# A graph network kernel: source table in four chunks instead of five, and layer 0 selecting ten columns of a block instead of eleven

## The chip, the cores and the metric

The kernel runs on one core of a Trainium2 chip. The metric is the device time of one execution in microseconds. Three runs of the kernel before gave 5798.82, 5797.19 and 5807.0 us, a median of 5798.82 us.

## The reference, cut to what matters

12,500 nodes carry 16 features each; 400,000 edges, sorted by destination, each name a source and a destination node. Two layers run one after the other, and both have the same skeleton: fetch the source row of every edge, turn it into a message, sum the messages by destination.

```
x  = layernorm(x + L0(x));  x = layernorm(x + L1(x))
L0: ew  = (edge_attr @ W_e + b_e).reshape(E, 16, 16)
    msg = einsum('ei,eio->eo', x[src], ew)
    out = segment_sum(msg, dst) / max(count, 1) + bias
L1: msg = einsum('emh,eh->em', edge_emb[edge_type], x[src])
    m   = segment_sum(msg, dst);  out = GRU(m, x)
```

## The kernel before, in words

The edges are worked in 125 blocks of 3200. A block is 25 columns of 128 edges, one edge to a partition. Each layer goes through all 125 blocks, and each block needs `x[src]` for its 25 columns. There are two ways of getting a column, and the kernel uses both at once.

A **gathered** column is one indirect DMA issued by GpSimd (POOL, line 500), 128 rows of 16 numbers straight into the tile `z`. In the kernel before 14 of the 25 columns are gathered.

A **selected** (or picked) column is computed. The node table lies in SBUF as a high and a low part (`table_hi`, `table_lo`), partition p holding the 98 nodes 98p to 98p+97, its groups. For each edge ScalarE (ACT) makes a one-hot column that says which partition holds the source: `dist` (line 570) is the absolute distance between the wanted partition number and the partition, `pick` (line 578) is relu(1 - dist). The 98 groups are cut into chunks of `NG` groups, and the one-hot is made once for every chunk, so that an edge outside a chunk contributes zero. TensorE (PE) multiplies the one-hots with the chunks (line 752), for each chunk once with the high and once with the low part, all accumulated in one PSUM bank: NG groups times 16 features. VectorE (DVE) multiplies that bank with a one-hot over the group inside the chunk (`select`, line 953, two columns at a time, output `cand`) and adds up along the groups (line 959), into `z`. `group_hot` (line 943) makes the group one-hot. Eleven columns of a block are selected, in the order of `PICKED`; ACT works them in two halves (`HCUT`), of 5 and 6 columns.

With the 25 source columns in `z`, DVE forms the outer products of the edges in three parts (`outer`, line 991, after columns 8, 15 and 25), PE sums them by destination in 50 matmul records (`sum_block`, line 789), ACT copies the sums (line 590), PE transposes them (lines 760 to 764), ACT copies again (lines 555, 557), PE multiplies by the weights (lines 770 to 773), and DVE adds the result to the node table by four small additions at addresses it loads into registers (`rows_of_windows`: load at 997, additions at 935).

The work of neighbouring blocks is woven by hand. While block b is summed, PE selects the columns of block b+1: in layer 0 it does columns 0 to 4, then `sum_block(b)`, column 5, the transposes, column 6, the result, and the rest; in layer 1 columns 0 to 2, `sum_block(b)`, 3, 4, the transposes, 5, 6, the result, and the rest (`S_AT`, `T_AT`, `R_AT`). The products go through a ring of six PSUM banks, so column t waits until DVE has taken the column six before it; columns 0 and 1 of the next block wait for the pair (6, 8) of this one. DVE in layer 0 runs, in this order: third outer product of b, pair (0,2) of b+1, the block's destination one-hot (`match_block`), pair (2,4) and its sum, first outer product of b+1, pair (4,6) and its sum, second outer product of b+1, register loads and additions for b, pair (6,8), pair (8,10) and their sum, the single column 10 and its sum, `group_hot`. Layer 1 is the same, with the second outer product after the additions.

The gathers are spread by hand too: `AFTER_OWN`, `AFTER_LAST` and `AFTER_SUMS` name the gathers of a block that wait until PE has finished a given column or `sum_block`.

Of the kernel before, what the change touches and what calls it, by code (L numbers as in the profile page):

```python
# [18 lines left out]
LN_AT = (0, 12, 34, 56, 78, 98)  # L19
N_LN = len(LN_AT) - 1  # L20
PICKED = [4, 5, 6, 7, 13, 14, 21, 22, 23, 24, 20]
H = ((11, 11), (11, 11))
HM = max(max(h) for h in H)
SCUT = [[[sum(p < START[j] for p in PICKED[:h]) for j in range(NS + 1)] for h in hs] for hs in H]
HCUT = [[(0, 5, h) for h in hs] for hs in H]
NH = 2
# [6 lines left out]
S_AT, T_AT, R_AT = (4, 2), (5, 4), (6, 6)  # L33
GATHERED = [[[[g for g in range(START[j], START[j + 1]) if g not in PICKED[:h]] for j in range(NS)] for h in hs] for hs in H]
assert all(2 * n % RING == 0 and n >= max(hs) for n, hs in zip(TURN, H))
HALF_1 = 5
MADE_0 = (H[0][0], HALF_1)
FIRST_GATHERED = [[[g for g in range(START[j], START[j + 1]) if g not in PICKED[m:h[0]]] for j in range(NS)] for m, h in zip(MADE_0, H)]
# [2 lines left out]
SUMMED = [(0, 4), (4, 6), (6, 10), (10, 11)]  # L41
assert all(PICKED[t] == PICKED[a] + t - a for a, b in SUMMED for t in range(a, b))
PAIRS = [[[(t, min(t + 2, h)) for t in range(0, h, 2)] for h in hs] for hs in H]
AFTER_OWN = ([{5: 0, 6: 1, 7: 2, 8: 3, 12: 5, 13: 6}] * 2, [{6: 0, 7: 1, 10: 3, 11: 4, 13: 5}] * 2)
AFTER_SUMS = (9, 8)
AFTER_LAST = ([{0: 7, 1: 8, 2: 9, 4: 10}] * 2, [{0: 7, 1: 8, 2: 9, 4: 10}] * 2)
SUB = 4
GPAD = -(-G // SUB) * SUB
WN = 32
TC, NG = 5, 20  # L50
CHUNKS = (0, 1, 4, 2, 3)
PER_ROW = 98
ROW_MUL, ROW_SHIFT = 2675, 17
NG_MUL, NG_SHIFT = 205, 12
NG_LAST = PER_ROW - (TC - 1) * NG
assert 0 < NG_LAST <= NG and NG_LAST % 2 == 0 and CHUNKS[0] != TC - 1 != CHUNKS[-1] and all(n * NG_MUL >> NG_SHIFT == n // NG for n in range(PER_ROW))
BLK = P * G
# [10 lines left out]
def build(nc, x, src, src_pick, dst, dst_rows_in, ea, etype, W_e, b_e, bias, A_t, w_ihT, w_hhT, b_ih, b_hh, out):  # L68
# [42 lines left out]
    with ExitStack() as ctx:  # L111
# [198 lines left out]
        def picked_of(k, buf, r, n):  # L310
            return ahead(k, buf, r) + H[k][1] + n

        def cand_of(k, buf, r, n):
            return ahead(k, buf, r) + RING + n
# [12 lines left out]
        def windows_of(eng, b):  # L327

            _, (n_win,) = nc.values_load_multi_w_load_instructions(
                span_row[0:1, bass.ds(b, 1), N_WIN:N_WIN + 1].rearrange("p a b -> p (a b)"), [eng.engine], min_val=0,  # L330
                max_val=N_MAX, skip_runtime_bounds_check_because="a count, worked out from the destinations")
            return n_win
# [149 lines left out]
        def _(pool):  # L482
            def gathers(k, table):
                l = L[k]

                def body(b, buf, r, columns):
# [3 lines left out]
                    for j in range(NS):  # L490
                        for g in columns[j]:
                            if b > 0:
                                if n in AFTER_OWN[k][buf]:
                                    pool.wait_ge(l["picked"], picked_of(k, buf, r, AFTER_OWN[k][buf][n] + 1))
                                if n in AFTER_LAST[k][buf]:
                                    pool.wait_ge(l["picked"], picked_of(k, 1 - buf, r - 1 + buf, AFTER_LAST[k][buf][n] + 1))
                                if n == AFTER_SUMS[k]:
                                    pool.wait_ge(l["mm"], b)
# [47 lines left out]
        def _(act):  # L546
            def evacuate(k):
# [11 lines left out]
                def pick_half(b, buf, r, j):  # L559

                    n, lo, hi = TC * (NH * b + j), HCUT[k][buf][j] * P, HCUT[k][buf][j + 1] * P

                    def distances():
                        if isinstance(b, int) and b == 0:
                            act.wait_ge(s_first, 32)
                        else:
                            act.wait_ge(l["src"][buf][j], 16 * (r + buf))
                        for i, c in enumerate(CHUNKS):
                            act.wait_ge(l["pick_act"], n + i + 2 - TC)
                            act.activation(dist[i][:, 0:hi - lo], src_mod[buf][:, lo:hi],  # L570
                                           ACT.Abs, bias=neg_node[:, c:c + 1]).then_inc(l["dist"], 1)

                    def picks(*turns):
                        for i in turns:
                            if i == 0:
                                act.wait_ge(l["picked"], picked_of(k, 1 - buf, r - 1 + buf, HCUT[k][1 - buf][j + 1]))
                            act.wait_ge(l["dist"], n + i + 1)
                            act.activation(pick[j][:, CHUNKS[i], 0:hi - lo], dist[i][:, 0:hi - lo], ACT.Relu,  # L578
                                           bias=1.0, scale=-1.0).then_inc(l["pick_act"], 1)

                    return distances, picks
# [10 lines left out]
                def first_sums(b):  # L592
                    act.wait_ge(l["mm"], b + 1)
                    sums_to_sbuf(l["mS"])

                def first_rows(b):
                    sums_to_rows(l["tp"], l["tS"], b)

                def sums_of_windows(n_win):
                    def window(x, q):  # L600
                        act.wait_ge(l["mm_x"], x + 2)
                        sums_to_sbuf(l["mS_x"])
                        sums_to_rows(l["tp_x"], l["tS_x"], x)

                    with act.If(n_win > 1):
                        for_each_window(act, n_win, extra, window)
# [21 lines left out]
                def body(b, buf, r):  # L628
                    more1 = not (isinstance(b, int) and b + 1 >= NB)
                    more2 = not (isinstance(b, int) and b + 2 >= NB)  # L630
                    n_win = windows_of(act, b)
                    if more1:
                        _, second = pick_half(b + 1, 1 - buf, r + buf, 1)
                    if more2:
                        distances, picks = pick_half(b + 2, buf, r + 1, 0)
                    if more1:
                        second(*range(TC))
                    if more2:
                        distances()
                        if k == 0:  # L640
                            picks(0, 1)
                    first_sums(b)
                    if more2:
                        picks(*((2,) if k == 0 else (0, 1)))
                    first_rows(b)
                    if more2:
                        picks(*((3, 4) if k == 0 else (2, 3, 4)))
                    if more2:
                        distances, _ = pick_half(b + 2, buf, r + 1, 1)
                        distances()  # L650
                    sums_of_windows(n_win)

                return begin, lambda: for_each_block(act, first_body, body)

            def h_to_rows():
# [72 lines left out]
        def _(pe):  # L728
            def sums(k):
# [7 lines left out]
                def pick_rows(b, buf, r, t):  # L737
# [5 lines left out]
                    else:  # L743
                        last = max(u for u in range(H[k][1 - buf]) if (u - t - TURN[k]) % RING == 0)
                        pe.wait_ge(l["cand"], cand_of(k, 1 - buf, r - 1 + buf, last + 1))
                    for i, c in enumerate(CHUNKS):
                        if at == 0:
# [587 lines left out]
```

## Time and profile before

| | us |
|---|---|
| median of three runs | 5798.82 |
| profiled execution, own time | 5833.2 |
| profiled execution, span | 5831.4 |
| PE busy | 5227.1 (90%) |
| PEld busy | 4693.1 (80%) |
| DVE busy | 4199.3 (72%) |
| ACT busy | 3891.8 (67%) |
| POOL busy | 3412.9 (59%) |

The profile is of one execution. PE is TensorE's matmuls and PEld its weight loads, which overlap the matmuls. "q" behind an engine's name is its sequencer. Layer 0 fills the span to about 2890 us, layer 1 runs from about 2970 us. "remote" in a wait, and "another core or an unknown queue" in the chain, is a release for which the profile found no finished instruction just before it.

### The profile page before, as it was taken

The page shows a single profiled execution, that of the slowest core. Times are in us where ns is not written, and L with a number is a line of the kernel's source. Part 1 is how long each engine was busy: PE and PEld are TensorE (multiplying, and loading weights), DVE is VectorE, ACT ScalarE, POOL GpSimd, SP SyncE. Part 2 cuts the span into 40 slices and gives each one's busy share as a digit, 9 for nine tenths or more (in the row PEclk, how much of TensorE's full clock was granted, in tenths as well). Part 3 has the DMA queues.
Part 4 walks back from the last instruction along what each step waited for, and adds up shares of the span by engine and source line. Part 5 has one row for each costly group of instructions (what it writes and reads, how often), then busy time and mean ns, then how long its engine had stood idle before and what let it go on. Part 6 is the DMA issues. An engine that isn't in the chain of part 4 may idle for free.

```text
span 5831.4 us, 131035 instructions
## 1 busy us (share of the span) xinstructions
PE 5227.1 (90%) x41758; PEld 4693.1 (80%) x41759; DVE 4199.3 (72%) x5387; ACT 3891.8 (67%) x5533; POOL 3412.9 (59%) x3559
## 2 busy tenths in 40 slices
PE   6999999999999999999978888888888888888887
PEld 5888888888888888888767878788877788788887
DVE  7878787778777788777856666666666666666666
ACT  6666676676666666666566666666666666666664
POOL 6555565555555555555555656655655655655554
PEclk9999999999999999999989999999999999998998
DMA  3111111111111111111111111111111111111110
GB/s 66 33 30 31 33 31 31 31 31 33 30 31 33 30 31 33 31 32 31 25 23 23 23 24 23 23 23 22 23 23 23 23 23 22 24 22 23 23 23 14
DMA packets 330970, 161.25 MB, mean 28 GB/s; under 512 B 193244, under 2 KB 330011, under 8 KB 330771
## 3 DMA queue, kind: packets, MB, share of 16 engines
q1 hardware_dynamic: 218224, 130.59, 9.3%
q0 software_dynamic: 112512, 29.03, 6.3%
q10 hardware_dynamic: 160, 0.80, 0.1%
q8 instruction: 27, 0.44, 0.0%
q14 instruction: 47, 0.39, 0.0%
HBM read 157.44 MB, written 2.66 MB: 27 GB/s over the span
## 4 chain that ended last, share of the span: by engine, by line
PE 63%; issue 15%; DVE 12%; another core or an unknown queue 6%; DVEq 4%; ACT 0%; DMA 0%; POOL 0%; SPq 0%; ACTq 0%
PE psN L752 46%; PE psM L789 15%; DVE cand L953 6%; DVEq L997 2%; DVE nodeT L935 2%; DVE z L991 2%; DVE z L959 1%; DVEq L934 1%; DVEq L952 0%; PE psN L893 0%; PE psM L764 0%; DVEq L958 0%; PE psM L773 0%; DVE grp_hot L943 0%
## 5 line engine op out<-in xcount | busy, mean ns | idle before, releaser
L752 PE MATMUL psN<-table_hi,pick 128*128 128x320 f32 (+1 forms) x13670 | 4080.1, 316 | 167.8 <-DVE cand L953 85.3
L752 PE MATMUL psN<-table_lo,pick 128*128 128x320 f32 (+1 forms) x13670 | 3987.4, 308 | 13.7 <-issue 13.7
L752 PEld LDWEIGHTS psN<-table_hi,pick 128*128 128x128 f32 x13670 | 2598.8, 190 | 306.4 <-issue 226.1
L578 ACT ACTIVATE pick<-dist 128x640 fp32r<-128x640 bf16 (+1 forms) x2485 | 1790.5, 784 | 1336.8 <-PE psN L752 852.8
L752 PEld LDWEIGHTS psN<-table_lo,pick 128*128 128x128 f32 x13670 | 2599.6, 190 | 21.6 <-issue 21.5
L500 POOL DMA_INDIRECT z<-in_x,idx x1761 | 1704.4, 968 | 1176.9 <-issue 417.4
L500 POOL DMA_INDIRECT z<-h_rows,idx x1755 | 1682.2, 959 | 1168.3 <-issue 403.7
L570 ACT ACTIVATE dist<-src_mod,neg_node 128x640 bf16<-128x640 uint16 (+1 forms) x2485 | 1972.6, 874 | 3.3 <-DMA src_mod<-src_mod_rows 3.3
L953 DVE TENSOR_TENSOR cand<-psN,grp_hot 128x640 f32<-128x640 f32 (+1 forms) x1492 | 1122.1, 765 | 1061.3 <-PE psN L752 482.7
L991 DVE TENSOR_TENSOR z<-psD,z 128x2048 f32<-128x2048 f32 (+1 forms) x750 | 1367.8, 1824 | 55.6 <-issue 31.5
L789 PE MATMUL psM<-z,onehot 128*32 128x273 f32 (+1 forms) x12500 | 904.4, 345 | 371.4 <-issue 327.0
L959 DVE TENSOR_REDUCE z<-cand 128x64 f32<-128x1280 f32 (+2 forms) x995 | 1064.5, 1070 | 85.6 <-DVE cand L953 0.5
L789 PEld LDWEIGHTS psM<-z,onehot 128*32 128x32 f32 x12500 | 484.4, 111 | 746.7 <-issue 643.3
L935 DVE TENSOR_TENSOR nodeT<-nodeT,psM 17x32 f32 (+1 forms) x1000 | 178.6, 179 | 383.7 <-remote 220.2
L590 ACT COPY sumS<-psM 128x273 f32<-128x273 f32 (+1 forms) x250 | 82.0, 328 | 407.9 <-PE psM L789 407.4
L968 DVE TENSOR_TENSOR onehot<-col_f,psD 128x800 f32<-128x800 f32 x250 | 244.7, 979 | 0.0
L555 ACT COPY sumT<-psM 128x384 f32<-128x384 f32 x125 | 60.2, 482 | 123.0 <-PE psM L761 121.2
L943 DVE TENSOR_TENSOR grp_hot<-col_f,grp 128x220 f32<-128x220 f32 x249 | 94.5, 379 | 0.2
L770 PE MATMUL psM<-sumT,W 128*128 128x128 f32 x500 | 76.0, 274 | 2.3 <-issue 1.7
L770 PEld LDWEIGHTS psM<-sumT,W 128*128 128x128 f32 x500 | 69.9, 190 | 2.7 <-issue 1.9
L973 DVE COPY psD<-eab 128x400 f32<-128x400 f32 x125 | 71.3, 570 | 0.0
L773 PE MATMUL psM<-sumT,A 128*128 128x128 f32 x250 | 48.1, 274 | 0.7 <-issue 0.4
(108 smaller groups left out, 734.3 us busy)
## 6 DMA issues: line engine op xcount, KB each, us to landing
src_mod<-src_mod_rows SPq DMA_DIRECT2D x249, 192.0 KB
src_mod<-src_mod_rows SPq DMA_DIRECT2D x248, 160.0 KB
z<-in_x,idx POOLq DMA_INDIRECT x1761
z<-h_rows,idx POOLq DMA_INDIRECT x1755
eab<-in_edge_attr SPq DMA_DIRECT2D x125, 200.0 KB
idx<-in_src SPq DMA_DIRECT2D x250, 12.5 KB
dstb<-in_dst SPq DMA_DIRECT2D x250, 14.0 KB
grp<-src_grp SPq DMA_DIRECT2D x249, 5.5 KB
```

The costliest lines, as they stand in the source:

```text
L500: pool.indirect_dma_start(xs[k][buf][:, g, :], None, table, bass.IndirectOffsetOnAxis(ap=idx[buf][:, g:g + 1], axis=0),).then_inc(l["got"] ...
L570: act.activation(dist[i][:, 0:hi - lo], src_mod[buf][:, lo:hi], ACT.Abs, bias=neg_node[:, c:c + 1]).then_inc(l["dist"], 1)
L578: act.activation(pick[j][:, CHUNKS[i], 0:hi - lo], dist[i][:, 0:hi - lo], ACT.Relu, bias=1.0, scale=-1.0).then_inc(l["pick_act"], 1)
L752: mm = pe.matmul(rows[:, :, 0:cells.shape[2]], pick[j][:, c, at:at + P], cells, start=(i == 0 and part == 0), stop=(i == TC - 1 and part = ...
L770: pe.matmul(psR[:, 0:P], W0[:, c, :], sumT[:, c, :], start=(c == 0), stop=False)
L789: mm = pe.matmul(psM[s * WN:(s + 1) * WN, 0:W], onehot[buf][:, g, :], z[k][buf][:, g, 0:W], start=(g == FIRST_POS[s]), stop=(g == LAST_POS ...
L935: return dve.tensor_tensor(v, v, psR[p0:p1, s * WN:(s + 1) * WN], ALU.add).then_inc(acc, 1)
L953: dve.tensor_tensor(cand[:, t0 - g0:t1 - g0], psN[:, a:a + m, 0:NG * F].rearrange("p m (f g) -> p m f g", g=NG), grp_hot[:, t0:t1, :].unsq ...
L959: dve.tensor_reduce(xs[k][buf][:, PICKED[t0]:PICKED[t1 - 1] + 1, :], cand[:, t0 - g0:t1 - g0], AX.X, ALU.add).then_inc(l["sel"], t1 - t0)
L968: return dve.tensor_tensor(onehot[buf][:], col_f[:, 0:WN].unsqueeze(1).to_broadcast([P, G, WN]), bc(rel[buf][:, 0:G], WN), ALU.is_equal)
L991: dve.tensor_tensor(z[k][buf][:, cs, 0:n * F].rearrange("p g (k i) -> p g k i", i=F), coef[k][buf][:, cs, :].unsqueeze(3).to_broadcast([P, ...
L997: _, vals = nc.values_load_multi_w_load_instructions(span_row[0:1, bass.ds(b, 1), 0:N_WIN + 1].rearrange("p a b -> p (a b)"), [dve.engine] ...
```

## The change

The 98 groups are cut into four chunks of 26, 26, 26 and 20 groups (before: four of 20 and one of 18), in the order 0, 3, 1, 2. Layer 0 selects the first ten columns of `PICKED` and gathers fifteen; layer 1 keeps eleven and fourteen. The points at which gathers wait follow the new counts. ACT's split of the chunks in layer 0 (before: two, one, two) becomes two, one, one.

```diff
-H = ((11, 11), (11, 11))
+H = ((10, 10), (11, 11))
-AFTER_OWN = ([{5: 0, 6: 1, 7: 2, 8: 3, 12: 5, 13: 6}] * 2, [{6: 0, 7: 1, 10: 3, 11: 4, 13: 5}] * 2)
-AFTER_SUMS = (9, 8)
-AFTER_LAST = ([{0: 7, 1: 8, 2: 9, 4: 10}] * 2, [{0: 7, 1: 8, 2: 9, 4: 10}] * 2)
+AFTER_OWN = ([{4: 0, 5: 1, 6: 2, 7: 3, 9: 4, 12: 5, 13: 6}] * 2, [{6: 0, 7: 1, 10: 3, 11: 4, 13: 5, 14: 6}] * 2)
+AFTER_SUMS = (10, 8)
+AFTER_LAST = ([{0: 7, 1: 8, 2: 9}] * 2, [{0: 7, 1: 8, 2: 9, 4: 10}] * 2)
-TC, NG = 5, 20
-CHUNKS = (0, 1, 4, 2, 3)
+TC, NG = 4, 26
+CHUNKS = (0, 3, 1, 2)
-NG_MUL, NG_SHIFT = 205, 12
+NG_MUL, NG_SHIFT = 158, 12
-                        picks(*((3, 4) if k == 0 else (2, 3, 4)))
+                        picks(*range(3 if k == 0 else 2, TC))
```

## Rows read from the trace of the kernel before

**Rows 1.** The page's chain that ended last, shares of the span.

```profile
PE 63%; issue 15%; DVE 12%; another core or an unknown queue 6%; DVEq 4%; ACT 0%; DMA 0%; POOL 0%; SPq 0%; ACTq 0%
```

**Rows 2.** Busy time in two stretches, layer 0 and layer 1.

```profile
100.00:2870.00 2770.00, 2613.36 (x20461) 2299.29 (x20460) 2205.44 (x2543) 1895.38 (x2662) 1634.79 (x1696) 1.00 0.17 31
3000.00:5780.00 2780.00, 2438.62 (x20010) 2243.68 (x20014) 1809.24 (x2579) 1850.55 (x2681) 1643.20 (x1715) 0.97 0.14 23
```

**Rows 3.** Waits, 200 to 2800 us: total us, times, longest.

```profile
POOL z L500 <- issue: 375.3, 1162, 2.7
...
DVE nodeT L935 <- remote: 191.8, 112, 2.5
DVE cand L953 <- remote: 135.5, 85, 2.6
```

**Rows 4.** Waits, 3100 to 5700 us.

```profile
DVE cand L953 <- remote: 189.6, 88, 2.8
...
PEld psM L789 <- DVE z L991: 35.9, 46, 0.9
...
PE psN L752 <- ACT pick L578: 24.3, 25, 1.1
```

**Rows 5.** Groups of instructions with shapes apart: busy us, mean ns.

```profile
L953 DVE TENSOR_TENSOR cand<-psN,grp_hot 128x640 f32<-128x640 f32 x1242 | 999.0, 820 | 1010.0 <-PE psN L752 458.0 <-remote 355.9 <-issue 195.3
...
L959 DVE TENSOR_REDUCE z<-cand 128x64 f32<-128x1280 f32 x497 | 739.0, 1487 | 51.1
...
L959 DVE TENSOR_REDUCE z<-cand 128x32 f32<-128x640 f32 x248 | 203.6, 821 | 25.9 <-DVE cand L953 0.5
...
L953 DVE TENSOR_TENSOR cand<-psN,grp_hot 128x320 f32<-128x320 f32 x250 | 123.0, 492 | 51.3 <-PE psN L752 24.7
```

**Rows 6.** The page's costliest groups: ACT's two steps and the gathers.

```profile
L578 ACT ACTIVATE pick<-dist 128x640 fp32r<-128x640 bf16 (+1 forms) x2485 | 1790.5, 784 | 1336.8 <-PE psN L752 852.8
L500 POOL DMA_INDIRECT z<-in_x,idx x1761 | 1704.4, 968 | 1176.9 <-issue 417.4
...
L570 ACT ACTIVATE dist<-src_mod,neg_node 128x640 bf16<-128x640 uint16 (+1 forms) x2485 | 1972.6, 874 | 3.3 <-DMA src_mod<-src_mod_rows 3.3
```

**Rows 7.** Timeline of layer 0, PE: start, duration; first matmuls of two neighbouring columns.

```profile
1506.30 0.31 PE L752 MATMUL psN<-table_hi,pick 128*128 128x320 f32 x1
...
1507.74 0.31 PE L752 MATMUL psN<-table_hi,pick 128*128 128x320 f32 x1
```

**Rows 8.** Timeline of layer 0, from column 5 to the next block's column 0.

```profile
1502.70 0.82 DVE L953 TENSOR_TENSOR cand<-psN,grp_hot 128x640 f32<-128x640 f32 x1 [0.91 <-PE psN L752]
...
1504.49 2.02 DVE L991 TENSOR_TENSOR z<-psD,z 128x1792 f32<-128x1792 f32 x1
...
1504.64 0.39 PE L771 MATMUL psM<-sumT,W 128*128 128x128 f32 x2
...
1508.65 1.13 DVE L935 TENSOR_TENSOR nodeT<-nodeT,psM 17x32 f32 x4 [2.14 <-remote]
...
1510.07 1.56 DVE L953 TENSOR_TENSOR cand<-psN,grp_hot 128x640 f32<-128x640 f32 x2 [0.29 <-issue]
...
1511.05 0.41 PE L752 MATMUL psN<-table_hi,pick 128*128 128x320 f32 x1 [0.26 <-DVE cand L953]
```

**Rows 9.** The block before: DVE's sequencer past its wait for the result (line 933).

```profile
L933 DVEq FUSED_REGOPS  x1: 46/46/46, 1485.2 to 1485.2; - x1
```

**Rows 10.** The same block: PE's sequencer at the next body's first register load.

```profile
L329 PEldq TENSOR_LOAD <-dst_mem x1: 305/305/305, 1485.3 to 1485.3; - x1
```

**Rows 11.** Timeline of a block in layer 1.

```profile
4479.77 0.41 PE L752 MATMUL psN<-table_hi,pick 128*128 128x320 f32 x1 [0.60 <-issue]
...
4484.82 0.42 PE L789 MATMUL psM<-z,onehot 128*32 128x128 f32 x8 [0.47 <-issue]
...
4489.34 0.41 PE L752 MATMUL psN<-table_hi,pick 128*128 128x320 f32 x1
...
4491.15 0.82 DVE L953 TENSOR_TENSOR cand<-psN,grp_hot 128x640 f32<-128x640 f32 x1 [3.19 <-PE psN L752]
...
4497.07 0.82 DVE L953 TENSOR_TENSOR cand<-psN,grp_hot 128x640 f32<-128x640 f32 x1 [2.25 <-remote]
```

## The prediction

> **What bounds the kernel now.** I read the chain that ended last first, then the busy times by layer, then the waits, then one block of each layer in order of time. In the chain PE has 63%, but DVE has 12% and 6% go to releases that the profile cannot name [rows 1]: a PE that was simply the limit would not need these. The busy times say which layer is which. A block of layer 0 has 169 matmul records (110 for the table, 50 sums, 9 behind them), so its stretch of 2770 us holds 20461/169 = 121.1 blocks of 22.88 us, with PE busy 21.6 and DVE 18.2 us of each; layer 1 has 163, hence 122.8 blocks of 22.64 us, with PE 19.9 and DVE 14.7 [rows 2]. PE is nearly full in layer 0, less so in layer 1.
>
> One block of layer 0 shows a loop. PE finishes column 5, DVE takes pair (4,6) at 1502.70, starts the second outer product at 1504.49, the additions at 1508.65, pair (6,8) at 1510.07, and only then, at 1511.05, may PE start column 0 of the next block [rows 8]. So the block is set by DVE's path behind column 5, not by PE's columns, which stop for 0.26 us there. Inside that path DVE stands idle 2.14 us before the additions although PE ended the result at 1504.64 + 0.39 = 1505.03 [rows 8]. This wait comes in nearly every block: 191.8 us over 112 times, and a second one ahead of a pair costs 135.5 us in 85 times [rows 3]. It looks as if the release of PE's semaphore came late. What it coincides with: in the block before, DVE got past the wait at 1485.2, and at 1485.3 PE's sequencer had run to the first register load of the next body [rows 9, 10]. I read this as: while PE's sequencer is pushing columns it lets no release out, and it lets them out when it has pushed the last one.
>
> The Trainium skill ("PSUM — Partial Sum Buffer", Engine vs sequencer instructions) says that an update attached to a matmul fires when that matmul completes. The rows disagree by 3.4 us in the place just shown. By that rule the additions would be held by something else, and fewer columns behind the result would not bring them forward.
>
> **The change part by part.**
>
> *PE, fixed cost of a matmul.* A column is ten matmuls and takes 1.44 us [rows 7]. It streams 98 groups x 16 x 2 = 3136 columns either way, 1307 ns at the granted clock of 1.00 (2.4 GHz) [rows 2]; the other 133 ns are 13 ns a matmul. Eight matmuls instead of ten save 0.027 us: 10 x 0.027 = 0.27 us a block in layer 0, 0.30 in layer 1. Bounds: nothing, if the 13 ns grow with width, and twice that.
>
> The Trainium skill ("TensorE: Matmul & The Clock Gate", Back-to-back issue gap) gives a fixed 2.5 ns for a warm matmul. By it the saving would be 0.05 us a block, some 13 us over both layers in place of 71; the row, 13 ns, is what I use.
>
> *PE, the eleventh column of layer 0* goes: 1.41 us more. Together 1.7 us a block, 212 us over 125 blocks, if PE were the only limit.
>
> *DVE, wider pairs.* A pair grows from 640 to 832 elements. From 492 ns at 320 and 820 at 640 the slope is 1.03 ns an element, so +0.20 us a pair; the sum of four columns goes from 1280 to 1664 elements at (1487 - 821)/640 = 1.04 ns, +0.40 us, that of two +0.20 [rows 5]. Layer 0: five pairs 0.99, sums 1.00, less the single column and its sum (0.49 + about 0.49): net +1.0 us a block. Layer 1: 1.09 + 1.10 = +2.2 us a block. `group_hot` adds under 0.1 us to either. DVE is then busy 19.2 of about 22 us, and 16.9.
>
> *ACT* makes two one-hots fewer a block, each 0.87 + 0.78 us: 3.3 us less of about 15 [rows 2, 6]. It pays where PE waits for ACT: 24.3 us in layer 1 [rows 4]. Elsewhere ACT waits for PE, and it is worth nothing.
>
> *POOL* issues one gather more in layer 0. A gather is 0.97 us and about 0.32 us to the next [rows 3, 6], so fifteen take 19.4 us of a block of about 22. The new waits tie it to PE columns, and the one on `sum_block` moves to the eleventh gather. With 2.6 us of slack I cost it at nothing; without that cover it would cost up to 1.3 us a block, 160 us. SP's loads are unchanged in number.
>
> **Sum for layer 0.** The path from column 5 to the next column 0 is 8.35 us (1502.70 to 1511.05), of which 2.14 is the late release. Three steps on it grow by 0.20: 8.95 us if the release stays where it is, 6.8 if it no longer counts. With the eleventh column gone PE's sequencer reaches the end of the body 1.4 us and more earlier, and DVE arrives 0.4 later, so I expect most of the 2.14 to vanish. PE itself needs for column 6, result and three columns 8.2 - 1.5 = 6.7 us, which meets the path at about the same point. That is worth 8.35 - 6.8 = 1.5 us. Against it stands the second late release, inside `sum_block`, 135.5 us in all [rows 3]: nothing in the change moves it, and behind it DVE has one pair and one four-column sum more to carry (+0.6). Between no gain (both releases stay) and 1.7 us (PE alone decides) I take 1.0 us: -125 us.
>
> **Sum for layer 1.** Here the sums wait for the third outer product: column 0 starts at 4479.77, the sums at 4484.82, though three columns need 4.3 us; the sums end at 4489.34, pair (2,4) follows at 4491.15, pair (4,6) at 4497.07 after a late release of 2.25 [rows 11]. So the loop is outer product, sums, column 3, DVE's whole remaining list, outer product. The 2.2 us of wider DVE work lie on it almost entirely. What can absorb them is the late release, 189.6 us in about 117 blocks, 1.6 us a block [rows 4], if it comes earlier or DVE simply arrives later. That leaves 2.2 - 1.6 = 0.6, less 0.2 for the waits for ACT [rows 4]: +0.4 us a block, +50 us. Bounds: -0.3 (PE's own saving, all else absorbed), -38 us, and +2.2, +275 us.
>
> Together 5833.2 - 125 + 50 = 5758 us for the profiled execution, which is 34.4 us above the median of the runs; **5724 us** as a median.
>
> **The rivals.**
>
> *A. PE's saving comes through whole.* Both late releases move with the shorter pushing of PE's sequencer, since every column has four instructions fewer in twenty. For it: PE is busy 94% in layer 0 [rows 2]. Against: DVE's path. Layer 0 -1.6 us a block, layer 1 none: -200 us, 5599.
>
> *B. Slower: DVE's list in layer 1 is the bound.* Mechanism: the loop through the third outer product and `sum_block`. For it: the sums already wait for DVE, 35.9 us in 46 times and the 0.47 us in [rows 4, 11]; all the 2.2 us are on the loop. It decides if the release ahead of pair (4,6) stays late relative to column 3, so that only the work in front of it hides: then +1.4 us a block, +175 us, while layer 0 keeps only 0.6 us, -75 us. Total +100: 5899. A lower clock adds to it: in layer 1, with PE busy 88%, the granted clock averages 0.97 against 1.00 in layer 0 at 94% [rows 2], and an emptier PE could be given that in layer 0 too.
>
> *C. The two layers cancel.* Layer 0 gains 0.6, layer 1 loses 0.6 us: 5799.
>
> **How the numbers follow.** Forecast 0.38, A 0.22, B 0.32, C 0.08. The predicted time is the forecast's, with a range of its own of 5670 to 5780. For 8 in 10 the range goes from just above the middle of A to the middle of B: 5595 to 5895. A measurement tells 0.2%, about 12 us, from no change. Faster: the forecast, A: 0.60. Same: 0.07. Slower: 0.33, B and the wrong side of C.
>
> **What would show it.** Pairs at about 1.02 us and four-column sums at 1.89 us confirm the DVE terms; a column at 1.41 us the PE term. In layer 0 the "remote" wait ahead of the additions should fall from 1.7 us a block to under 0.5, and the block to about 21.9 us. In layer 1 the wait of the sums for the outer product should grow and the block be about 23.0 us. The forecast is wrong if the remote waits of layer 0 stay, if POOL's gathers hold an outer product, or if the granted clock in layer 0 drops below 0.97.

## The result, and the profile after

The changed kernel takes 5827.73 us (median of 17 runs, 5820.51 to 5837.6) and the kernel before 5807.0 us beside it (median of 17, 5795.6 to 5823.21). The ratio is 1.0031, with a 95% interval of 1.0021 to 1.0041: slower by 0.3%, little but clear of the noise. Forecast were 5724 us and a chance of 0.33 for slower; the time lies inside the range for 8 in 10 (5595 to 5895) and outside the forecast's own (5670 to 5780). The profiled execution took 5832.04 us (span 5830.2), the one before 5833.2, so the two profiles show how time moved between the layers, and not the 0.3%.

| | before | after |
|---|---|---|
| median | 5807.0 | 5827.73 |
| PE busy | 5227.1 | 5078.8 |
| DVE busy | 4199.3 | 4598.4 |
| ACT busy | 3891.8 | 3059.0 |
| POOL busy | 3412.9 | 3503.1 |
| layer 0, us a block | 22.88 | 23.41 |
| layer 1, us a block | 22.64 | 22.10 |

The chain that ended last, answering to [rows 1]: less of it is without a name, more is PE.

```profile
PE 69%; DVE 14%; issue 13%; DVEq 2%; another core or an unknown queue 1%; ACT 1%; POOL 0%; DMA 0%; ACTq 0%; SPq 0%
```

The busy times by layer, answering to [rows 2]. The first row is layer 0, the second layer 1; the columns are the stretch, its length, then PE, PEld, DVE, ACT and POOL busy with their counts, the granted clock, the DMA share and GB/s.

```profile
100.00:2800.00 2700.00, 2436.09 (x16031) 1984.56 (x16029) 2214.05 (x2191) 1367.39 (x2072) 1642.59 (x1728) 0.99 0.16 30
...
3050.00:5700.00 2650.00, 2291.54 (x16910) 2088.43 (x16910) 2031.54 (x2522) 1472.90 (x2162) 1609.56 (x1684) 0.99 0.14 24
```

A block of layer 0 now has 80 + 50 + 9 = 139 matmul records, so the stretch of 2700 us holds 16031/139 = 115.3 blocks of 23.41 us; one of layer 1 has 88 + 53 = 141, hence 119.9 of 22.10 us. Layer 0 lost 0.53 us a block and layer 1, which was to lose, won 0.54. All block times below come from such a row in the same way (169 and 163 records with five chunks).

The groups with shapes apart, answering to [rows 5], and PE's columns, answering to [rows 7] (total and mean ns stand behind the bar).

```profile
L752 PE MATMUL psN<-table_hi,pick 128*128 128x416 f32 x7830 | 2862.0, 366 | 248.1 <-DVE cand L953 139.0 <-DVEq L920 37.3 <-ACT pick L578 37.1
...
L953 DVE TENSOR_TENSOR cand<-psN,grp_hot 128x832 f32<-128x832 f32 x1242 | 1247.5, 1020 | 869.0 <-PE psN L752 605.2 <-remote 151.9 <-issue 100.8
...
L959 DVE TENSOR_REDUCE z<-cand 128x64 f32<-128x1664 f32 x497 | 937.8, 1887 | 51.2
```

```profile
1500.68 0.31 PE L752 MATMUL psN<-table_hi,pick 128*128 128x320 f32 x1
...
1502.14 0.31 PE L752 MATMUL psN<-table_hi,pick 128*128 128x320 f32 x1
```

DVE's pairs are 1.02 us and its four-column sums 1.89, as the prediction had them. A column takes 1502.14 - 1500.68 = 1.46 us, where the prediction had 1.41 and the kernel before 1.44.

The waits from 200 to 2750 us, answering to [rows 3], which go to 2800 us; the sums' wait of the kernel before, over the same 2550 us, stands in the second fence.

```profile
ACT sumS L590 <- PE psM L789: 502.9, 103, 6.5
...
PEld psM L789 <- issue: 377.6, 640, 1.3
...
DVE cand L953 <- PE psN L752: 334.1, 215, 4.2
...
PE psM L789 <- issue: 142.6, 261, 1.0
...
PE psN L752 <- issue: 29.7, 60, 1.1
...
DVE nodeT L935 <- remote: 8.0, 26, 1.0
DVE cand L953 <- remote: 3.9, 4, 1.5
```

```profile
PEld psM L789 <- issue: 256.3, 475, 1.3
```

The two late releases of layer 0 did go: 191.8 + 135.5 us before, 11.9 after. But the block did not get shorter. The time stands inside `sum_block` (line 789), where PE now stops between matmuls for "issue", with nothing before it that the profile names as a cause. One block of layer 0 in order of time, answering to [rows 8]:

```profile
1488.42 4.54 PE L789 MATMUL psM<-z,onehot 128*32 128x273 f32 x47
...
1489.40 0.95 POOL L500 DMA_INDIRECT z<-in_x,idx  x1 [1.71 <-PE psN L752]
...
1490.66 0.95 POOL L500 DMA_INDIRECT z<-in_x,idx  x1 [0.30 <-issue]
1490.81 0.11 PEld L789 LDWEIGHTS psM<-z,onehot 128*32 128x32 f32 x1 [0.41 <-issue]
1491.54 0.16 PEld L789 LDWEIGHTS psM<-z,onehot 128*32 128x32 f32 x5 [0.62 <-issue]
1491.92 0.95 POOL L500 DMA_INDIRECT z<-in_x,idx  x1 [0.30 <-issue]
1492.29 0.15 PEld L789 LDWEIGHTS psM<-z,onehot 128*32 128x32 f32 x4 [0.60 <-issue]
...
1493.04 0.11 PEld L789 LDWEIGHTS psM<-z,onehot 128*32 128x32 f32 x1 [0.59 <-issue]
1493.18 0.95 POOL L500 DMA_INDIRECT z<-in_x,idx  x1 [0.30 <-issue]
1493.75 0.65 PE L789 MATMUL psM<-z,onehot 128*32 128x273 f32 x3 [0.79 <-issue]
```

The reader is to see four gathers issued while PE sums, and PE's weight loads that come in small groups with about 0.6 us of nothing between them. The 50 records fill 1488.42 to 1494.40. From here on "sums" is the time from the first matmul of line 789 to the first matmul behind `sum_block`, a mean over the blocks of a layer that I worked out from PE's records; so is the number of gathers issued from 1 us before them to 1 us before their end, called the gathers beside the sums. In layer 0 the sums went from 5.19 to 6.62 us (mostly three gathers before, mostly four after); in layer 1 they went from 4.26 to 2.92 us (two gathers, then one).

### The profile page after: what moved, and what is told of

The parts are those of the page before. It is cut to its first block, busy times and chain, and to the rows that moved or that the text cites. A ratio compares the mean times of both kernels' runs of the same rounds, so it can differ in the third digit from the quotient of the medians.

```text
span 5830.2 us, 115014 instructions
## 1 busy us (share of the span) xinstructions
PE 5078.8 (87%) x35298; PEld 4369.0 (75%) x35299; DVE 4598.4 (79%) x5139; ACT 3059.0 (52%) x4539; POOL 3503.1 (60%) x3683
## 4 chain that ended last, share of the span: by engine, by line
PE 69%; DVE 14%; issue 13%; DVEq 2%; another core or an unknown queue 1%; ACT 1%; POOL 0%; DMA 0%; ACTq 0%; SPq 0%
PE psN L752 50%; PE psM L789 16%; DVE cand L953 6%; DVE z L991 3%; DVE z L959 2%; PE psM L770 1%; DVE nodeT L935 1%; DVEq L997 1%; ACT pick L578 1%; PE psM L760 0%; PE psM L771 0%; DVEq L934 0%; DVE grp_hot L943 0%; DVEq L952 0%
## 5 line engine op out<-in xcount | busy, mean ns | idle before, releaser
L752 PE MATMUL psN<-table_hi,pick 128*128 128x416 f32 x10440 | 3632.2, 351 | 250.1 <-DVE cand L953 139.0
L752 PE MATMUL psN<-table_lo,pick 128*128 128x416 f32 x10440 | 3577.7, 347 | 18.0 <-issue 18.0
L500 POOL DMA_INDIRECT z<-in_x,idx x1885 | 1799.2, 954 | 1149.8 <-PE psN L752 471.7
L752 PEld LDWEIGHTS psN<-table_hi,pick 128*128 128x128 f32 x10440 | 1977.5, 189 | 445.7 <-issue 253.8
L578 ACT ACTIVATE pick<-dist 128x768 fp32r<-128x768 bf16 (+1 forms) x1988 | 1397.3, 757 | 1486.4 <-PE psN L752 1285.5
L752 PEld LDWEIGHTS psN<-table_lo,pick 128*128 128x128 f32 x10440 | 1983.0, 190 | 66.6 <-issue 25.3
L953 DVE TENSOR_TENSOR cand<-psN,grp_hot 128x832 f32<-128x832 f32 x1368 | 1322.1, 981 | 885.7 <-PE psN L752 606.9
L570 ACT ACTIVATE dist<-src_mod,neg_node 128x768 bf16<-128x768 uint16 (+1 forms) x1988 | 1531.8, 842 | 3.7 <-DMA src_mod<-src_mod_rows 3.7
L959 DVE TENSOR_REDUCE z<-cand 128x32 f32<-128x832 f32 (+2 forms) x871 | 1264.9, 1452 | 81.0
L943 DVE TENSOR_TENSOR grp_hot<-col_f,grp 128x286 f32<-128x286 f32 (+1 forms) x249 | 108.8, 437 | 0.2
```

The source lines that it names most:

```text
L500: pool.indirect_dma_start(xs[k][buf][:, g, :], None, table, bass.IndirectOffsetOnAxis(ap=idx[buf][:, g:g + 1], axis=0),).then_inc(l["got"] ...
L752: mm = pe.matmul(rows[:, :, 0:cells.shape[2]], pick[j][:, c, at:at + P], cells, start=(i == 0 and part == 0), stop=(i == TC - 1 and part = ...
L943: dve.tensor_tensor(grp_hot[:, 0:H[k][buf], :], col_f[:, 0:NG].unsqueeze(1).to_broadcast([P, H[k][buf], NG]), bc(grp[buf][:, 0:H[k][buf]], ...
L953: dve.tensor_tensor(cand[:, t0 - g0:t1 - g0], psN[:, a:a + m, 0:NG * F].rearrange("p m (f g) -> p m f g", g=NG), grp_hot[:, t0:t1, :].unsq ...
L959: dve.tensor_reduce(xs[k][buf][:, PICKED[t0]:PICKED[t1 - 1] + 1, :], cand[:, t0 - g0:t1 - g0], AX.X, ALU.add).then_inc(l["sel"], t1 - t0)
```

## The experiments

Theory after the result: indirect gathers that run beside PE's work hold PE up, and the fifteenth gather of layer 0, which was costed at nothing, eats what the dropped column brings. It is theory G in e4 to e8 and theory 1 from e9 on; theory 1 of e1 and e2 says only that the missing column makes the sums slow. The rivals changed as the runs came in; each expectation names its own.

**One half at a time.** *e1: four chunks, eleven columns and fourteen gathers kept in both layers.*

```diff
-H = ((10, 10), (11, 11))
+H = ((11, 11), (11, 11))
```
(with layer 0's waiting points of the kernel before)

> Four chunks of 26, 26, 26, 20, but eleven selected and fourteen gathered columns in layer 0, as before. In the changed kernel a layer 0 block is 23.44 us (22.88 before), its sum_block 6.6 us (5.2 before); a layer 1 block 22.08 (22.62 before). Theory 1, the missing eleventh column makes the layer 0 sums slow (less other work between two sum_blocks): sums back to about 5.2 us, layer 0 block at most 22.9, total about 5740 us. Theory 2, the wider matmuls of the four chunks do it: sums stay at 6.5 us, layer 0 block about 24.5, total about 5940 us.

Measured 5740.57 us, ratio 0.9893 (0.9878 to 0.9908): faster than both kernels. Its two layers:

```profile
100.00:2700.00 2600.00, 2483.86 (x16843) 2130.52 (x16842) 2335.42 (x2405) 1458.34 (x2061) 1530.06 (x1603) 1.00 0.17 32
3050.00:5700.00 2650.00, 2298.45 (x16905) 2091.78 (x16904) 2030.56 (x2521) 1462.72 (x2143) 1605.30 (x1675) 0.99 0.15 23
```

16843/147 gives blocks of 22.69 us in layer 0 (-0.19 against before), 16905/141 blocks of 22.10 in layer 1 (-0.54, all that the changed kernel has there). So the four chunks are a gain in both layers, and the sums of layer 0 are back at 5.4 us. Theory 1 was right here in sums and time.

*e2: five chunks, ten columns and fifteen gathers in layer 0.*

```diff
-H = ((11, 11), (11, 11))
+H = ((10, 10), (11, 11))
```
(in the kernel before, with the changed kernel's waiting points for layer 0)

> Five chunks of 20 and 18 as before, but ten selected and fifteen gathered columns in layer 0 with the new gather waits. Layer 1 is that of before, 22.6 us a block. Theory 1 (the missing column slows the sums): sums 6.5 us, layer 0 block 23.2 us or more, total about 5850 us. Theory 2 (the wide matmuls do it): sums 5.2 us, layer 0 block about 21.9 us, total about 5690 us.

Measured 5939.55 us, ratio 1.0227 (1.0207 to 1.0247).

```profile
100.00:2700.00 2600.00, 2261.98 (x17157) 1936.67 (x17157) 1858.45 (x2051) 1572.63 (x2376) 1541.02 (x1619) 0.97 0.16 29
```

17157/159 gives 24.1 us a block: 1.2 more than before, with a column less. The swap of a selected for a gathered column is the part that loses. The sums are 6.4 us, as theory 1 had it; the time is 90 us above its figure.

**Is it the gathers?** *e4: the changed kernel with layer 0's gathers replaced by a small fill of the same columns (this leaves out layer 0's gathered rows); e9: the same in the kernel before.*

```diff
+if k == 0:
+    pool.memset(xs[k][buf][:, g, :], 0.5).then_inc(l["got"][buf][j], 16)
+    continue
 pool.indirect_dma_start(
```

> The changed kernel, in layer 0 each gather replaced by a small constant fill on GpSimd with the same waits and the same semaphore, so no gather DMA runs in layer 0; layer 0 gets constant rows instead of the gathered ones. If the extra gather's traffic slows the sums (theory G), sum_block falls to 5 us or less and the total to about 5680 us. If not, sum_block stays above 6 us and the total within 40 us of the changed kernel's.

> The kernel before, with layer 0's gathers replaced by a small fill of the same columns (leaves out layer 0's gathered rows). Theory 1 (what holds PE beside the gathers is the gathers themselves, and the fifteenth is what ate the column): sum_block takes 3.3 us instead of 5.2, the late releases of layer 0 vanish, and the block is PE's own work, one column of 1.44 us above the 20.1 us of the same trial on the changed kernel: 21.4 us instead of 22.88, so about -180 us, 5625. The gathers then cost 1.5 us a block in the kernel before and 3.3 us in the changed one. Rival (the gathers cost the same in both, the changed kernel loses elsewhere): a block of about 19.6 us, 5410.

Measured 5402.84 us (e4, one run) and 5458.19 us (e9, ratio 0.9426, 0.9409 to 0.9442). Of e4 the first row is layer 0, the second the sums in one block's timeline; the last fence is e9's layer 0.

```profile
100.00:2500.00 2400.00, 2304.14 (x16614) 1996.80 (x16616) 2270.36 (x2270) 1418.52 (x2149) 170.08 (x1791) 1.00 0.12 28
```

```profile
1452.54 3.41 PE L792 MATMUL psM<-z,onehot 128*32 128x273 f32 x50
```

```profile
100.00:2500.00 2400.00, 2400.00 (x19916) 2180.11 (x19915) 2140.93 (x2475) 1829.31 (x2591) 161.96 (x1649) 1.00 0.12 30
```

Without gathers the 50 matmuls of a sum are one unbroken run: sums of 3.34 us in either kernel, and no late release is left in layer 0's waits. The blocks are 20.08 us (16614/139) and 20.37 us (19916/169). Three things follow. The gathers cost 2.5 us a block in the kernel before and 3.3 in the changed one; the late releases and the stops inside the sums go and come with them. In the kernel before PE is then busy 2400 of 2400 us, and a block is its own work. And one column less, together with four chunks for five, brings only 0.3 us even where no gather disturbs: in e4 DVE is busy 2270 of 2400 us, 95%, and PE waits for it. Theory 1 said 21.4 us for e9 and its rival 19.6; the truth lies between, because the column is not worth its 1.44 us. The fill also takes POOL's own work away (170 us busy in e4's stretch), so these two runs do not say whether a gather's issue or its traffic is what holds PE.

**Moving the gathers.** *e5 and e6: the changed kernel, fewer gathers beside the sums of layer 0; e8: the same as e6 in e1; e7: the kernel before with one more.*

```diff
-AFTER_SUMS = (10, 8)
+AFTER_SUMS = (9, 8)    # e5;  e6: (8, 8);  e8: e1 with (8, 8);  e7: before, (9, 8) to (10, 8)
```

> The changed kernel with one number other: in layer 0 the tenth gather of a block, not the eleventh, is the first to wait for sum_block, so that one gather less is issued beside the sums (three for four). Theory G (a gather issued beside sum_block costs PE about 1.4 us there): sums fall from 6.6 to about 5.2 us, a layer 0 block from 23.4 to about 22.1, the total to about 5670 us. Rival P (fifteen gathers are simply too many for GpSimd, or the later gather holds an outer product): total 5810 us or more.

> The changed kernel with the ninth gather of a layer 0 block as the first to wait for sum_block: two gathers beside the sums. Theory G: sums about 4.1 us, a block about 21.3 unless VectorE binds (20.7 us of work and gaps), total about 5600 us. Rival P: the ninth gather is the last that the second outer product needs, so VectorE waits for it and the total is above that of the run with three gathers beside the sums.

> The kernel before, nothing changed but that in layer 0 the eleventh gather, not the tenth, is the first to wait for sum_block: fourteen gathers as before, one more of them beside the sums. Theory G: sums from 5.2 to about 6.6 us, total about 5980 us. Rival P (the number of gathers counts, not their place): 5805 us, as before, or less, since GpSimd is done earlier.

> Four chunks, eleven selected columns in both layers, and the ninth gather of a layer 0 block as the first to wait for sum_block. Against the same kernel with the tenth (5740.6 us). Theory G: sums 5.4 to about 4.1 us, total about 5620 us unless VectorE binds. Rival P: 5740 us or more.

| | us | ratio (interval) | block | sums |
|---|---|---|---|---|
| e5 | 5907.88 | 1.0176 (1.0161 to 1.0192) | 24.1 | 5.02 |
| e6 | 5891.02 | 1.0163 (1.0138 to 1.0188) | 23.9 | 3.37 |
| e7 | 5827.70 | 1.0036 (1.0020 to 1.0053) | 23.1 | 6.03 |
| e8 | 5887.21 | 1.0140 (1.0124 to 1.0156) | 23.9 | 5.59 |

Moving gathers out of the sums does shorten the sums, to 3.37 us in e6 with two gathers beside them in every block, and the block gets longer all the same. Theory G was wrong in the time of all four. For e7 it had 5980 us: the sums grew by 0.84 us, the block by 0.2 only, and by my count the move put a fourth gather beside the sums in just 18 of 103 blocks. Rival P was right that e5, e6 and e8 get slower, but not in why: in e5 and e6 no wait of DVE ahead of an outer product (line 991) is listed, and e6 is not above e5. The gathers that went later run beside the last columns, and something else is held up there. A block of e6 in order of time:

```profile
1499.17 0.95 POOL L500 DMA_INDIRECT z<-in_x,idx  x1 [2.07 <-PE psM L789]
...
1506.72 0.95 POOL L500 DMA_INDIRECT z<-in_x,idx  x1 [0.30 <-issue]
1509.31 1.96 DVE L953 TENSOR_TENSOR cand<-psN,grp_hot 128x832 f32<-128x832 f32 x2 [2.39 <-remote]
1509.42 2.62 ACT L578 ACTIVATE pick<-dist 128x640 fp32r<-128x640 bf16 x4 [4.53 <-remote]
1510.00 0.95 POOL L500 DMA_INDIRECT z<-in_x,idx  x1 [2.33 <-remote]
...
1510.48 0.71 PE L752 MATMUL psN<-table_hi,pick 128*128 128x416 f32 x1 [3.16 <-DVE cand L953]
...
1512.57 0.55 PE L752 MATMUL psN<-table_hi,pick 128*128 128x416 f32 x1
1512.91 0.55 PE L752 MATMUL psN<-table_lo,pick 128*128 128x416 f32 x1
...
1514.31 0.35 PE L752 MATMUL psN<-table_lo,pick 128*128 128x416 f32 x1
1514.50 0.35 PE L752 MATMUL psN<-table_hi,pick 128*128 128x416 f32 x1
```

PE had ended its columns 3.16 us before 1510.48, at 1507.3, and DVE, ACT and POOL, which waited for just these, went on at 1509.3, 1509.4 and 1510.0. PE was idle, so it was pushing nothing: this refutes my reading of the late release. What stands before it is a row of seven gathers without a pause, from 1499.17 to the last at 1506.72.

The rows show a second cost, which I had overlooked. After the idle 3.16 us PE goes on at its lower clock: from matmul to matmul 1512.91 - 1512.57 = 0.34 us, and 0.19 from 1514.31 on. The row of that stretch, the granted clock behind POOL's count:

```profile
1510.40:1513.50 3.10, 3.02 (x9) 2.92 (x10) 3.00 (x3) 3.10 (x6) 2.45 (x3) 0.50 0.29 60
```

The granted clock of layer 0 is 0.93 in e6, 0.96 in e5, 0.97 in e2 and 0.89 in e3, against 1.00 before and 0.99 in the changed kernel. By my count of the steps from one column matmul to the next that are about twice their usual length, the lower clock adds 1.2 us a block to PE's work in e6, 0.8 in e5 and 0.6 in e2, and 0.1 in the changed kernel, where before had 0.2. So part of what e2, e5 and e6 lose is clock, and no run here parts it from the rest; the changed kernel's own loss is not.

*e3: the changed kernel, `sum_block` after column 2 instead of after column 4.*

```diff
-S_AT, T_AT, R_AT = (4, 2), (5, 4), (6, 6)
+S_AT, T_AT, R_AT = (2, 2), (5, 4), (6, 6)
```

> The changed kernel with layer 0's sum_block moved from behind column 4 to behind column 2, so that PE reaches it before the third outer product is there and has to wait, as it does in layer 1. If the sums are slow because PE's instructions come too slowly and a wait lets them pile up (theory S), sum_block falls to about 3 us, the layer 0 block to about 22.0 and the total to about 5660 us. If the sums are slowed by what runs beside them, they stay at 6 us, the wait comes on top, and the total is 5900 us or more.

Measured 6160.06 us, ratio 1.0611 (1.0592 to 1.0629), 26.1 us a block. The sums are 3.34 us in every block, with one or two gathers beside them, and PE waits 4.35 us for DVE ahead of column 0 instead (374.4 us in 86 times), at a granted clock of 0.89. So theory S was right in the sums and wrong in the time, its rival the other way round. That gathers beside the sums cost nothing there, as in e6, would fit a supply of instructions that runs short only where PE has not waited before. Against so simple a rule stands e5, where PE waits 2.3 us ahead of column 0 (215.5 us in 95 times) and the sums still take 5.0 us.

**One gather less.** *e10 and e11: the changed kernel without the gather of column 20 (the last of a block) or of column 15 (the tenth); each leaves out that column's source rows. The count that the outer product waits for is one lower too.*

```diff
+if k == 0 and b > 1 and g == 20:    # e11: g == 15
+    continue
 pool.indirect_dma_start(
```

> The changed kernel without the gather of column 20, layer 0's fifteenth in a block and its last (leaves out that column's source rows, which keep old values); all else is unchanged, so PE selects ten columns and POOL issues fourteen gathers. Theory 1 (each gather beside PE's work costs it 1.3 to 1.5 us wherever it lies): layer 0's block 23.44 -> 22.0 us, -175 us, 5650. Rival A (only gathers beside sum_block cost anything): this one lies beside columns, no change, 5825. Rival B (the loss is in DVE's wider pairs, not in the gathers): no change either, 5825.

> The changed kernel without the gather of column 15, the tenth in a block, which is issued while PE sums (leaves out that column's source rows). Theory 1 (each gather costs 1.3 to 1.5 us wherever it lies): sum_block 6.6 -> 5.2 us, the block 22.0 us, 5650. Rival A (only gathers beside sum_block cost anything): the same 5650, but then the trial without the last gather shows no change. Rival B (DVE's wider pairs are the bound): sum_block gets shorter, but the block stays within 0.3 us of 23.4, about 5810.

Measured 5701.57 us (ratio 0.9850, 0.9834 to 0.9867) and 5692.13 us (0.9841, 0.9820 to 0.9862). Layer 0 of e10, then of e11:

```profile
100.00:2700.00 2600.00, 2397.76 (x16106) 1989.36 (x16106) 2223.99 (x2201) 1375.91 (x2086) 1545.90 (x1623) 0.98 0.17 30
```

```profile
100.00:2700.00 2600.00, 2394.78 (x16185) 2007.33 (x16177) 2230.22 (x2211) 1381.60 (x2095) 1548.59 (x1629) 0.99 0.17 31
```

22.44 and 22.33 us a block: the fifteenth gather costs 0.97 to 1.08 us, and which one goes makes hardly a difference to the block. It does to where the time comes from: the sums fall from 6.6 to 6.1 us in e10 and to 5.6 in e11, so all of it stands inside the sums in e11 and about half in e10. Both rivals fall. The expected gain was a little too large (22.0 us a block). With e1 this splits the swap: from eleven columns to ten with fourteen gathers, 22.69 to 22.4, brings 0.3 us; the fifteenth gather then takes 1.0. The sum is +0.7 us a block.

**Other exchanges.** *e12: e1 with ten columns and fifteen gathers in layer 1; e13: with twelve and thirteen in layer 1; e14: with twelve and thirteen in layer 0.*

```diff
-H = ((11, 11), (11, 11))
+H = ((11, 11), (10, 10))    # e12;  e13: ((11, 11), (12, 12));  e14: ((12, 12), (11, 11))
-PICKED = [4, 5, 6, 7, 13, 14, 21, 22, 23, 24, 20]
+PICKED = [4, 5, 6, 7, 13, 14, 21, 22, 23, 24, 19, 20]    # e13, e14
```
(cut: the waiting points follow the counts, and in e13 and e14 the last pair and its sum have two columns)

> Four chunks in both layers, eleven selected columns and fourteen gathers in layer 0, ten and fifteen in layer 1. Theory 1 (a column selected less relieves DVE's loop, a gather more costs 1.0 to 1.1 us where it runs beside PE's work): in layer 1 DVE's path through the third outer product is the loop, the single column and its sum are 1.2 us of it (0.59 + 0.59), and one gather more costs about 1.05 us of PE, which waits for DVE there 2.6 us a block anyway: layer 1 from 22.04 to about 21.3 us a block, -90 us against the four chunks alone, 5650. Rival (one column for one gather is a loss in either layer, as in layer 0 with +0.73 us a block): 22.8 us, +90 us, 5830. A result near 5740 says that the two cancel in layer 1.

> Four chunks, layer 0 with eleven selected and fourteen gathered, layer 1 with twelve and thirteen (the opposite swap). Theory 1 (a gather beside PE's work costs 1.0 to 1.1 us a block, and a column selected less is worth little because DVE's path takes it back): in layer 1 the loop through the third outer product is DVE's, and the twelfth column adds 0.43 us to a pair and 0.43 to a sum on it, while the thirteenth to fourteenth gather goes, which costs PE little where PE waits for DVE: layer 1 22.04 -> 22.5 us, +55 us against the four chunks alone, 5795. Rival (gathers are dearer than columns in either layer, as both swaps so far said, +0.73 and +1.65 us a block): 21.5 us, -65 us, 5675.

> Four chunks, layer 0 with twelve selected and thirteen gathered, layer 1 with eleven and fourteen. PE's own work in layer 0 is 20.5 us a block without gather traffic (kernel before), so 22.0 with a twelfth column; DVE's is 19.4 + 0.85 = 20.3. Theory 1 (a gather costs 1.0 us of PE): 22.0 + the stall of thirteen gathers. Fourteen cost 2.4 us in the kernel before, so thirteen 1.3 to 1.4: 23.3 us against 22.71, +75 us, 5815. Rival (the price of a gather is not linear: the last one costs 1.0 because it falls beside the sums, the others cost nothing like it): 24.2 us, +180 us, 5920.

Measured 5962.52 us (e12, ratio 1.0247, 1.0222 to 1.0272), 5644.96 us (e13, 0.9734, 0.9706 to 0.9762) and 5727.73 us (e14, 0.9895, 0.9878 to 0.9911). Layer 1 of e12; layers 0 and 1 of e13; layer 0 of e14 and one block's sums in it:

```profile
3050.00:5700.00 2650.00, 2186.39 (x14890) 1940.19 (x14891) 1751.37 (x2124) 1279.34 (x2016) 1607.15 (x1679) 0.93 0.13 21
```

```profile
100.00:2700.00 2600.00, 2525.84 (x17104) 2181.18 (x17106) 2377.27 (x2443) 1478.64 (x2090) 1546.62 (x1627) 1.00 0.17 32
3050.00:5600.00 2550.00, 2349.42 (x17438) 2226.54 (x17437) 2070.92 (x2457) 1526.80 (x2102) 1454.09 (x1522) 0.98 0.14 25
```

```profile
100.00:2700.00 2600.00, 2542.69 (x17841) 2263.76 (x17839) 2428.86 (x2417) 1557.86 (x2073) 1426.79 (x1498) 1.00 0.16 33
```

```profile
1457.03 3.41 PE L789 MATMUL psM<-z,onehot 128*32 128x273 f32 x50 [0.43 <-issue]
```

With four chunks, from these rows (records of a block: 133, 141, 149 in layer 1; 139, 147, 155 in layer 0):

| selected / gathered | layer 0 block | sums | layer 1 block | sums |
|---|---|---|---|---|
| 10 / 15 | 23.41 | 6.62 | 23.67 | 5.67 |
| 11 / 14 | 22.69 | 5.39 | 22.10 | 2.92 |
| 12 / 13 | 22.59 | 3.40 | 21.79 | 1.96 |

The rival of e12 and e13 was right in the direction, and I was wrong in both: in layer 1 too a gather is dearer than a column, although PE waits for DVE there. The rival's size was too small in e12 (22.8 us for 23.67). There the granted clock is 0.93 against 0.99 in e1, and the same count gives 1.1 us a block of slow matmul steps, so how much of the 1.57 us is the gather and how much the clock stays open.

In layer 0 the twelfth column came far cheaper than either theory said (22.6 for 23.3 and 24.2). With thirteen gathers POOL is through before PE sums in most blocks (87 of 125 have none beside the sums), and the 50 matmuls run unbroken. So a gather's price depends on how many there are. An estimate: PE's own work is 19.3 us a block in e4 (2304.14 us busy in 119.5 blocks) and 22.2 with two columns of 1.46 us more, so thirteen gathers cost some 0.4 us here, and fifteen cost 3.3.

e13 is 2.7% faster than the kernel before, some 3% faster than the changed one, and faster than e1. Some of its gain is not explained: its layer 0 is e1's but for the eleventh selected column (19 for 20), and the block is 2600/(17104/147) = 22.35 us and not 22.69. By my count mostly two gathers are issued beside the sums there and mostly three in e1, and the sums are 5.2 and 5.4 us; that is 0.2 of the 0.34. Against that layer 0, e14's twelfth column is a loss of 0.24 us, so in layer 0 it is open whether the twelfth column for the fourteenth gather pays.

## Why the prediction was wrong, point by point

**The step that failed: "With 2.6 us of slack I cost it at nothing".** The fifteenth gather costs 0.97 to 1.08 us a block in layer 0 (e10, e11), some 125 us (110 and 119 us by the totals, each against the kernel before in the same series). The bound given beside it (up to 1.3 us, 160 us) was about right, but I had it as POOL's own time, and POOL has slack. What pays is PE: the gathers stop it, inside `sum_block` above all (6.62 us for 5.19). The trace of before showed a sign of it that I did not use: the sums' weight loads wait 256.3 us for "issue" from 200 to 2750 us of the kernel before, in 475 places, with three gathers beside them. The prediction named "POOL's gathers hold an outer product" as what would break it; no wait of DVE ahead of line 991 is listed in layer 0 of the changed kernel, and they held PE instead.

**"The eleventh column of layer 0 goes: 1.41 us more."** As PE work right; as time 0.3 us, with gathers (e1 against e10, e11); without them, e9 against e4 gives 0.3 us for the column and the chunks together. In the sum for layer 0 I had taken 1.0 of 1.7 us, because DVE's path from column 5 on sets the next column 0. It takes more than I gave it.

**"Eight matmuls instead of ten save 0.027 us."** Failed with its sign: a 416-wide matmul is followed by the next after 190 ns (median), a 320-wide one after 147. Over 173 and 133 ns of columns at 2.4 GHz the extra is 17 and 14 ns, so it grows with width, which was the lower bound of that term. The column went from 1.44 to 1.46 us, which is the median over layer 0 too, so on its mean a 416-wide matmul takes (1460 - 2 x 147)/6 = 194 ns. The Trainium skill ("TensorE: Matmul & The Clock Gate", Back-to-back issue gap) gives its 2.5 ns for an isolated matmul; no row here shows so little.

**"Most of the 2.14 to vanish."** It did: 191.8 us to 8.0, and the second one, of which I had said that nothing moves it, from 135.5 to 3.9. This gave nothing, because the sums took as much again (5.19 to 6.62 us); that it is one and the same delay is not shown. It came true by luck, as the reason given for it was wrong. **"While PE's sequencer is pushing columns it lets no release out"** was wrong: in e6 the release is 2 us late behind an idle PE, and without gathers (e4, e9) there is no such wait at all in layer 0, with more pushing and not less. Nor does the coincidence of [rows 9, 10] hold in the very block of [rows 8]: there DVE's sequencer is past its wait 0.5 us before PE's comes to the next body.

```profile
L933 DVEq ALU_OP  x1: 40/40/40, 1508.5 to 1508.5; - x1
```

```profile
L329 PEldq TENSOR_LOAD <-dst_mem x1: 303/303/303, 1509.0 to 1509.0; - x1
```

The Trainium skill's rule ("PSUM — Partial Sum Buffer", Engine vs sequencer instructions) is that the update fires when the matmul completes. In e4 and e9 the trace agrees, with no such wait in layer 0; beside gathers e6 shows the update reach three engines 2 us or more late.

**DVE's terms** were right to the hundredth (1.02, 1.89 us). **ACT's** saving was worth nothing in layer 0, as said; the 0.2 us a block booked for it in layer 1 did not come, as PE's waits for ACT there are 21.2 us after and 24.3 before. **Layer 1** had the wrong sign: forecast +0.4 us a block, measured -0.54, although DVE's 2.2 us are all there (14.7 to 16.9 us busy a block). The step was "+50 us", a sum in which the late release could absorb 1.6 us and no more. The waits of layer 1 that bear on it, first from 3100 to 5700 us of before, as [rows 4], then from 3050 to 5700 us of after:

```profile
PE psM L789 <- DVE z L991: 23.7, 46, 0.6
...
DVE nodeT L935 <- remote: 11.6, 6, 2.3
```

```profile
DVE cand L953 <- remote: 131.1, 99, 5.4
...
PE psM L789 <- DVE z L991: 121.2, 89, 4.2
...
DVE nodeT L935 <- remote: 41.7, 48, 1.2
```

The wait of the sums for the outer product did grow, as forecast, by 0.8 us a block. But the sums themselves fell by 1.3 us (4.26 to 2.92), with one gather beside them instead of two, and this term the prediction did not have at all. The two together are the -0.54. DVE's release waits fell too, from 201 to 173 us. (In [rows 11] the 0.47 us ahead of the sums is an "issue", and not a wait for DVE, as rival B read it.) That the wider work moved PE against POOL's gathers is what the counts say; I have no run that moves only that in layer 1, so the cause of its gain stays argued.

**The sum.** Layer 0: -0.3 for the column, +1.0 for the gather, -0.2 for the chunks: +0.5 a block. Layer 1: -0.54. The layers nearly cancel, as rival C had it, though from opposite signs, and the time lies 0.3% above. Rival B named slower, but through DVE's list in layer 1, which did not decide. C's total of 5799 us came within 29 us by luck, and so did B's direction.

## What to carry to other kernels

Before a transfer is costed at nothing because its issuing engine has slack, look at what the busiest engine does while it runs: short matmuls with idle time "issue" beside gathers are a price that is paid already, and one gather more raises it. Replace the transfers by a fill once: that one run gives the whole price of the gathers, issue and traffic (here 2.5 us of 22.9 a block), and what is left as the bound. And a wait that vanishes is no gain until the block is shorter. Moving gathers only moved the stall between the sums and the releases, and where PE then stood idle its clock fell as well; the fastest run (e13, 2.7%) has four chunks and one gather less in layer 1, and part of its gain is not explained.

## What the runs showed of the hardware

Indirect gathers slow a stream of short matmuls on PE that doesn't depend on them: in layer 0, 50 matmuls with their weight loads take 3.34 us where no gather runs (e4, e9), 5.2 with mostly three beside them (before), 6.8 with four (106 blocks of the changed kernel), in stops of about 0.6 us. The long matmuls of the columns show few such stops (29.7 us in all, against 142.6 inside the sums). With gathers, releases of PE's semaphores can reach DVE, ACT and POOL some 2 us late, even when PE is idle (e6); without them this is gone from layer 0 (e4, e9). What the common cause is (the supply of instructions, or the path of the releases, or the table's weight loads) stays open: the runs take gathers away or move them, and none separates these. Nor is the price a clean function of the number beside the sums: e8 has mostly two there and 5.6 us, e6 has two and 3.37, e3 one or two and 3.34, the blocks of layer 0 of the changed kernel with three have 5.1.

Where PE stood idle for 3.16 us it went on at the lower of its two clock levels (granted 0.50 from 1510.40 to 1513.50 in e6): a 416-wide matmul then follows the last after 0.34 us instead of 0.19.

Two layers 0 that differ in which column is gathered last (e13 gathers 20 and selects 19, e1 the other way round) differ by 0.34 us a block. I have no reason for it that explains all of it.
